# Who splits the softmax weights into high and low parts: ScalarE, GpSimd and VectorE in a two-layer attention kernel

## The reference, cut to what matters

```python
x = x + conv_attention(group_norm(x))      # layer 0: 6 heads of 64, relative positions by row and column
t = tokens(x)
t = t + causal_attention(layer_norm(t))    # layer 1: 6 heads of 64
t = t + ffn(layer_norm(t))                 # 384 -> 1536 -> 384, exact gelu, weights are Kronecker products
# both attentions, per head:
#   w = softmax(q @ k.T * scale + bias_or_mask);  out = w @ v;  then one output projection
```

## Time and profile before

| | |
|---|---|
| median of 3 runs | 3036.42 us (3030.33 to 3038.16) |
| the profiled execution, its own time | 3037.59 us |
| its span, first to last instruction | 3035.9 us |
| mean granted TensorE clock | 0.957 of full speed |
| busy share: PE, PEld, DVE, ACT, POOL | 89%, 52%, 73%, 58%, 59% |
| length of one image in the steady state | about 372 us |

### The profile page before, as it was taken

One profiled execution on the slowest core, in us unless ns is written; L12 is line 12 of the kernel. 1 busy time (PEld: TensorE's weight loads), 2 busy tenths in 40 slices (PEclk: granted clock), 3 DMA queues, 4 the chain that ended last, 5 costly groups with the idle time before them and its releaser, 6 DMA issues.

```text
span 3035.9 us, 68416 instructions
## 1 busy us (share of the span) xinstructions
PE 2700.3 (89%) x29020; PEld 1576.3 (52%) x29020; DVE 2223.7 (73%) x3769; ACT 1767.0 (58%) x2091; POOL 1781.9 (59%) x1181
## 2 busy tenths in 40 slices
PE   5899888999889988899989999899988999889995
PEld 3455544556446563465635655355553655535562
DVE  6786868767777777867777687686876868767684
ACT  5565645646556566564565655656555565555563
POOL 5374764737547375583756746466464665647464
PEclk8999999999999999999999999899999999999998
DMA  3000001000100001000010000100001000010000
GB/s 118 22 2 1 2 22 43 2 1 2 43 22 2 1 2 43 22 2 1 2 43 22 2 1 2 54 11 2 1 2 63 2 2 1 2 43 2 2 2 22
DMA packets 32751, 48.11 MB, mean 16 GB/s; under 512 B 5152, under 2 KB 32032, under 8 KB 32448
## 3 DMA queue, kind: packets, MB, share of 16 engines
q1 hardware_dynamic: 30944, 43.13, 4.3%
q10 hardware_dynamic: 1504, 0.61, 0.1%
HBM read 30.95 MB, written 12.58 MB: 14 GB/s over the span
## 4 chain that ended last, share of the span: by engine, by line
PE 42%; DVE 21%; POOL 16%; issue 13%; ACT 7%; DMA 0%; POOLq 0%; DVEq 0%; SPq 0%; ACTq 0%
PE ps L547 10%; POOL pl L995 8%; PE ps L881 6%; POOL ph L1038 5%; DVE mxp L951 5%; PE ps L671 4%; PE ps L842 4%; PE ps L851 4%; PE ps L806 4%; DVE pl L995 3%; ACT qa L655 2%; DVE stats L1115 2%; PE ps L844 2%; DVE x L1111 2%; PE ps L1090 2%
## 5 line engine op out<-in xcount | busy, mean ns | idle before, releaser
L995 POOL TENSOR_TENSOR pl<-p,ph 128x1024 f16<-128x1024 f32 x336 | 822.7, 2448 | 406.0 <-ACT ph L928 381.6
L951 DVE TENSOR_REDUCE mxp<-ps 128x1 f32<-128x512 f32 (+2 forms) x1344 | 777.4, 626 | 180.0 <-PE ps L806 172.2
L926 ACT ACTIVATE p<-ps 128x1024 f32<-128x1024 f32 (+1 forms) x672 | 644.1, 960 | 450.4 <-PE ps L851 444.1
L881 PEld LDWEIGHTS ps<-v,ph 128*128 128x128 f16 x9600 | 517.7, 98 | 133.0 <-issue 42.6
L995 DVE TENSOR_TENSOR pl<-p,ph 128x1024 f16<-128x1024 f32 (+1 forms) x336 | 426.5, 1269 | 214.4 <-POOL ph L1038 209.2
L881 PE MATMUL ps<-v,ph 128*128 128x65 f16 (+1 forms) x9600 | 541.9, 195 | 22.7 <-DVE pl L995 14.9
L881 PE MATMUL ps<-v,pl 128*128 128x65 f16 x4800 | 519.3, 194 | 0.0
L881 PEld LDWEIGHTS ps<-v,pl 128*128 128x128 f16 x4800 | 452.8, 100 | 0.0
L851 PE MATMUL ps<-qc,kc 65*128 65x512 f16 (+3 forms) x1344 | 388.5, 371 | 0.0
L686 POOL TENSOR_TENSOR v<-o,v 128x384 f16<-128x384 f32 x128 | 113.2, 889 | 444.6 <-ACT o L682 444.6
L928 ACT ACTIVATE ph<-p 128x1024 f16<-128x1024 f32 x336 | 355.2, 1057 | 10.7
(11 more groups left out here) (189 smaller groups left out, 5244.7 us busy)
## 6 DMA issues: line engine op xcount, KB each, us to landing
xin<-in_x SPq DMA_DIRECT2D x8, 1536.0 KB, 7.0
x<-in_x SPq DMA_DIRECT2D x8, 1536.0 KB, 8.0
out<-x SPq DMA_DIRECT2D x16, 768.0 KB, 3.6
qc<-rowt SPq DMA_DIRECT2D x96, 2.0 KB
o<-in_L_conv_qkv_w SPq DMA_DIRECT2D x2, 576.0 KB, 10.3
p<-in_L_conv_qkv_w SPq DMA_DIRECT2D x1, 576.0 KB, 11.4
x<-in_L_attn_Wq SPq DMA_DIRECT2D x1, 576.0 KB, 12.1
x<-in_L_attn_Wk SPq DMA_DIRECT2D x1, 576.0 KB, 13.0
```

The source lines that it names most:

```text
L881: mm = nc.tensor.matmul(m.ps[:, 6 + half % 2, c0:c0 + w], e, v, start=(first and n == 0), stop=(g in self.last_of_half and n == len(work) ...
L926: nc.scalar.activation(m.p32[:, i % RING, :, 0:w], m.ps[:, 2 * (i % 2):2 * (i % 2) + 2, 0:w], ACT.Exp, scale=SCALE).then_inc(s["exp"], 1)
L951: nc.vector.reduce_max(m.mxp[:, h % 2, kh, qt:qt + 1], m.ps[:, bank, 0:w], AX.X).then_inc(s["free"], 1)
L995: engine.tensor_tensor(m.pl[:, i % RING, :, 0:w], m.p32[:, i % RING, :, 0:w], m.ph[:, i % RING, :, 0:w], ALU.subtract).then_inc(sem, 1)
```

## The change

ScalarE makes the high part of every group. GpSimd makes the low part of all of an even group and of the first key tile of an odd group. VectorE makes the low part of the second key tile of an odd group. The semaphores `hi_act` and `hi_pool` become one, `hi`; readers of an odd group's low part wait for `pl_pool` and for `pl_dve`.

```diff
     def wait_hi(self, eng, i):
-        name = "hi_act" if self.even(i) else "hi_pool"
-        eng.wait_ge(self.s[name], self.s.at(name, i // 2 + 1))
+        eng.wait_ge(self.s["hi"], self.s.at("hi", i + 1))
     def wait_lo(self, eng, i):
-        name = "pl_pool" if self.even(i) else "pl_dve"
-        eng.wait_ge(self.s[name], self.s.at(name, i // 2 + 1))
+        eng.wait_ge(self.s["pl_pool"], self.s.at("pl_pool", i + 1))
+        if not self.even(i):
+            eng.wait_ge(self.s["pl_dve"], self.s.at("pl_dve", i // 2 + 1))
...
-    def high_part(self, eng, i, copy, sem):
+    def high_part(self, act, i):
...
-        copy(m.ph[:, i % RING, :, 0:w], m.p32[:, i % RING, :, 0:w]).then_inc(sem, 1)
+        self.nc.scalar.activation(m.ph[:, i % RING, :, 0:w], m.p32[:, i % RING, :, 0:w], ACT.Copy).then_inc(self.s["hi"], 1)
...
-            if self.even(i):
-                self.high_part(act, i, lambda out, in_: nc.scalar.activation(out, in_, ACT.Copy), s["hi_act"])
+            self.high_part(act, i)
...
-    def low_part(self, eng, engine, i, sem):
+    def low_part(self, eng, engine, i, sem, part):
...
-        engine.tensor_tensor(m.pl[:, i % RING, :, 0:w], m.p32[:, i % RING, :, 0:w], m.ph[:, i % RING, :, 0:w], ALU.subtract).then_inc(sem, 1)
+        engine.tensor_tensor(m.pl[:, i % RING, part, 0:w], m.p32[:, i % RING, part, 0:w], m.ph[:, i % RING, part, 0:w], ALU.subtract).then_inc(sem, 1)
...
-                self.low_part(dve, self.nc.vector, i - 1, self.s["pl_dve"])
+                self.low_part(dve, self.nc.vector, i - 1, self.s["pl_dve"], 1)
...
-            if self.even(i):
-                self.low_part(pool, nc.gpsimd, i, self.s["pl_pool"])
-            else:
-
-                self.high_part(pool, i, lambda out, in_: nc.gpsimd.tensor_scalar(out, in_, 1.0, 0.0, ALU.mult, ALU.add), self.s["hi_pool"])
+            self.low_part(pool, nc.gpsimd, i, self.s["pl_pool"], slice(0, 2) if self.even(i) else 0)
```

More of the change, by code:

```diff
@@ L693 @@
 class Attention:
-    COUNTS = (dict(scores=48, exp=48, hi_act=24, hi_pool=24, pl_dve=24, pl_pool=24, pv=48, use=116, free=116, combined=6, nm=6, row=96, recip=12,
+    COUNTS = (dict(scores=48, exp=48, hi=48, pl_dve=24, pl_pool=48, pv=48, use=116, free=116, combined=6, nm=6, row=96, recip=12,
                    out=12, ot_hi=6),
-              dict(scores=36, exp=36, hi_act=18, hi_pool=18, pl_dve=18, pl_pool=18, pv=36, use=84, free=84, combined=6, nm=6, row=96, recip=12,
+              dict(scores=36, exp=36, hi=36, pl_dve=18, pl_pool=36, pv=36, use=84, free=84, combined=6, nm=6, row=96, recip=12,
                    out=12, ot_hi=6))
@@ L905, in tensor @@
         self.use(pe, self.tail[1])
-    def high_part(self, eng, i, copy, sem):
+    def high_part(self, act, i):
         m, w = self.m, self.cols(i)
-        eng.wait_ge(self.s["exp"], self.s.at("exp", i + 1))
+        act.wait_ge(self.s["exp"], self.s.at("exp", i + 1))
         if i >= RING:
-            eng.wait_ge(self.s["pv"], self.s.at("pv", i - RING + 1))
-        copy(m.ph[:, i % RING, :, 0:w], m.p32[:, i % RING, :, 0:w]).then_inc(sem, 1)
+            act.wait_ge(self.s["pv"], self.s.at("pv", i - RING + 1))
+        self.nc.scalar.activation(m.ph[:, i % RING, :, 0:w], m.p32[:, i % RING, :, 0:w], ACT.Copy).then_inc(self.s["hi"], 1)
     def ot_high(self, act, u):
```

## The result

The changed kernel takes 2981.11 us (median of six runs; one of the six, at 3863.61 us, was disturbed), and the kernel before, run beside it, 3033.05 us. The ratio is 0.984, with a 95% interval of 0.982 to 0.986. That is 51.9 us less, where I forecast 27.5. The span of the profiled execution fell by 57.5 us, from 3035.9 to 2978.4, and the mean granted clock rose from 0.957 to 0.968.

What follows compares the result with a forecast made beforehand. TensorE was taken as the bound, losing 126 us waiting for VectorE, itself held up by GpSimd. Terms of -3.3 us in seven images and -4.4 in the last gave -27.5 from 3037.6, 3010.1, as median 3009; range 2978 to 3048.

Steps and rivals of the forecast that it cites:

- steps 13 and 21: Layer 0, each with a row behind an odd low part: VectorE's shorter low part saves 2 x 0.54, -1.1 us.
- step 3: Layer 0, TensorE waiting on VectorE: half of the odd low part leaves VectorE, saving 0.54 us.
- steps 5 and 6: Layer 0: line 988 no longer waits behind GpSimd's high part before step 5's row, 1.0 us; clock 1.7 more as bound.
- the units: Layer 0: the copy of line 405 starts 0.37 us later behind the high part, six times an image, +2.2 us.
- steps 27 to 36: Layer 0's normalisation: ScalarE becomes the bound at 5.55 us a pair, 28.35 us against 27.36, +1.0 us.
- step 37: Layer 0, step 37 to 38: the row is done in time, 6.25 us becomes 4.18, -2.1 us.
- steps 38 to 46: Layer 0's last head: exponential and high part on ScalarE take 2.03 us, TensorE's own pace, so priced at nothing.
- layer 1, first two heads (steps 0 to 11): The low part no longer waits for a high part from an occupied GpSimd: -2.0 us, bounds 0 and -3.
- layer 1, last heads: ScalarE's added high parts cost time, half of 1.9 us of waiting for VectorE's low part goes: +0.2 us.
- rival (b): Row stalls vanish: half of TensorE's 126 us of waits for VectorE and the slow clock stretch go; 2983 us, chance 0.17.
- rival (c): VectorE and GpSimd start an odd group's halves together, VectorE is held 1.06 us; slower, 3046, at worst 3083; chance 0.18.
- (d): GpSimd's even low part still holds the row; gains fail, ScalarE's costs come: 3047 us, or 3039; chance 0.20.

Runs made afterwards that it cites:

- unit_first: The changed kernel, with ScalarE's copy of a unit moved ahead of the odd group's high part: 2943.32 us, 0.971 of the kernel before; run again, 2939.70 us.
- group5: The kernel before, with only the high part of group 5 in layer 0 moved from GpSimd to ScalarE: 3020.74 us, 0.996 of before.
- layer1_only: The kernel before, with the whole change made in layer 1 alone: 3013.83 us, 0.994 of before.
- hi_only: The changed kernel, with odd low parts whole on VectorE as before; ScalarE still makes all high parts: 3011.92 us, 0.993 of the kernel before.
- pool_all: The changed kernel, with all low parts on GpSimd and none on VectorE: 3004.13 us, 0.992 of the kernel before.
- norm_pool: unit_first, with layer 0's high parts of groups 27, 29, 31, 33, 35 on GpSimd and their low parts whole on VectorE: 2988.38 us, 0.987 of before.

## Why the prediction was right, and where it was wrong

The direction was right, the size was not: 52 us less against 27.5, and 2981 us against 3009. That 2981 is just inside the range (2978 to 3048) is luck, as two errors of opposite sign met. One step failed in kind: steps 13 and 21, -1.1 in the sum, measured +3.2. Without this loss (unit_first) the time is 2943, far under the range. The other terms came out 8 us an image better than the sum had them, mostly because it left the slow stretches behind steps 5 and 37 out of the sum (2.6 us), took layer 1's gain too low (1.9), had the stages between the attentions at nothing (1.5) and charged steps 27 to 36 for what they didn't cost (1.0). Term by term, in us of a steady image:

| term of the sum | forecast | measured |
|---|---|---|
| step 3 | -0.54 | -0.53 |
| steps 5 and 6 | -1.0 | -2.7 |
| steps 13 and 21 | -1.1 | +3.2 |
| the units | +2.2 | +1.7 |
| steps 27 to 36 | +1.0 | 0.0 |
| step 37 | -2.1 | -2.55 |
| steps 38 to 46 | 0 | -1.1 |
| layer 1, first two heads (steps 0 to 11) | -2.0 | -3.3 |
| layer 1, steps 12 to 26 | 0 | -0.6 |
| layer 1, last heads | +0.2 | +0.2 |
| the stages between the attentions | 0 | -1.5 |

**Step 5, and its clock.** The cause was right: group5 moves that one high part and gets step 5 at 4.48 us and step 6 at 2.47. Mis-sized was the rest of the term: I named the slow stretch of the earlier trace rows as a bound, 1.7 us, and left it out of the sum. It came: 1.0 and 1.7 are the 2.7 measured. The timeline and the window after the change:

```profile
856.06 2.13 POOL L994 TENSOR_TENSOR pl<-p,ph 128x1024 f16<-128x1024 f32 x1 [1.36 <-ACT ph L912]
...
856.61 1.60 DVE L985 TENSOR_TENSOR mxp<-mxp 128x8 f32<-128x8 f32 x1
858.24 0.17 DVE L987 TENSOR_SCALAR nm<-mxp 128x8 f16<-128x8 f32 x1
...
859.06 0.22 PE L811 MATMUL ps<-ident,nm 128*8 128x128 f16 x1 [1.30 <-DVE mxp L950]
...
853.00:863.00 10.00, 8.70 (x103) 5.07 (x102) 7.72 (x13) 6.35 (x7) 5.06 (x5) 1.00 0.01 2
```

VectorE's combination still waits behind GpSimd's even low part (1.60 us), as rival (b)'s counter-argument had it, but the scaling no longer waits (0.17). TensorE stands 1.30 us instead of 1.87, and the granted clock over the 10 us is 1.00, so all of it at 2.4 GHz, instead of 0.83. Step 6 falls from 3.64 us to 2.47 by this. The same holds of step 38 (2.86 to 2.00), behind the stop of step 37, which I hadn't priced at all; there the granted clock had also been 0.83 over 10 us before the change. That a shorter stop keeps the clock up is read from these places. The length of one stop doesn't settle it, as step 21 shows.

**Steps 13 and 21.** This step of the prediction failed. I subtracted 0.54 us twice and wrote against rival (c) that the maxima ahead of the low part in VectorE's queue let GpSimd's half get well ahead. GpSimd's half was not the danger, but its next even low part, 2.14 us. Before, VectorE had started ahead of it by 0.28 us, and my own term for the units, 0.37 us later, was larger than this lead. I had priced that shift for TensorE's maxima alone and not carried it on to VectorE's low part.

The hold costs 1.4 us in step 13 (3.84 to 5.23 in six images) and 1.4 in step 21 (3.95 to 5.34). In four images step 21 took a further 1.4 to 1.7 us at the lower clock: of the windows below, the third image's and the fourth's, the first is at 0.83 and the second at 1.00, though TensorE had stopped for 1.97 us in both. That was one of my signs of being wrong, a new stop with a low clock behind it. In the third image step 13 fell instead, from 7.47 us. unit_first gives all of this back.

```profile
903.00:913.00 10.00, 8.03 (x79) 4.59 (x77) 6.91 (x11) 5.16 (x7) 3.29 (x2) 0.83 0.01 3
1267.70:1277.70 10.00, 8.03 (x103) 5.21 (x102) 8.56 (x13) 6.57 (x8) 3.29 (x2) 1.00 0.01 2
```

So rival (c) is real at two steps an image, by another partner than the one it named, and it is nowhere near deciding the sign.
The Trainium skill, page "SBUF — State Buffer", section "Who interferes with whom", says that the order of issue decides who is blocked. By that rule the trace agrees: VectorE 0.07 us behind took 2.62 us, and 0.06 us ahead took 0.69.

**The units.** The copy came 0.36 us later (0.37 forecast). Five of the six even steps behind it took 0.34 us more; step 14 has nothing waiting and took the same (2.54, 2.55).

**Steps 27 to 37.** ScalarE did become the bound; its timeline in steps 33 to 35, and the window over steps 33 to 36, after the change:

```profile
946.24 0.80 ACT L460 ACTIVATE lT<-xin,small 128x512 f32<-128x512 f32 x1
947.07 0.63 ACT L466 ACTIVATE xin<-lT 128x512 f16<-128x512 f32 x1
947.60 1.01 ACT L926 ACTIVATE p<-ps 128x1024 f32<-128x1024 f32 x1
948.64 1.06 ACT L912 ACTIVATE ph<-p 128x1024 f16<-128x1024 f32 x1
949.60 1.00 ACT L926 ACTIVATE p<-ps 128x1024 f32<-128x1024 f32 x1
...
944.00:954.00 10.00, 10.00 (x137) 6.42 (x135) 7.82 (x14) 9.82 (x12) 9.69 (x7) 1.00 0.01 2
```

The mechanism was right, the term too large. Neighbouring instructions of ScalarE can overlap in the records: the exponential at 949.60 starts 0.10 us before the high part ahead of it ends, so a high part adds less than its 1.06 us. From one exponential to the next it is 2.00 us, and an odd step takes 3.37 us where I had added a full 1.06 to 2.46 and got 3.52. A pair is 5.37 us where I had 5.55, and the ten steps take 27.34 us (27.37 before). Steps 37 and 38 gained as TensorE had the row ready in time; the row of step 37 waits for nothing after the change. Steps 39 to 46 go at ScalarE's pace of 2.00 instead of 2.03.

**Layer 1.** Both the low part that came late and its wait were right, but I read one instance and took its 1.95 us, where the first two heads held more such steps: they fell from 24.03 to 20.67 us. This is above my upper bound of 3. layer1_only shows that this gain stands by itself, and hi_only (20.62 us for these steps) that it comes from the high part and not from the split. VectorE's low part waited 209 us for GpSimd's high part before, over the whole span, and now waits 183 us for ScalarE's, so the waits of VectorE in total don't show this gain; the steps do.

**The stages between** gave 0.3 to 1.1 us an image that I had at nothing. No experiment takes them apart. In layer1_only the part from layer 0 to layer 1 is absent, so it hangs on layer 0's half of the change; more isn't shown.

**The rivals.** The time fell on rival (b)'s 2983, and partly for its reason: the four waits of the earlier trace rows for VectorE's maxima, scaling and low part, 126 us, are down to 73, and the clock held at step 5. But the row stalls of steps 13 and 21 got longer and were not gone; with unit_first, where they take 3.7 us each, the time is 2943, and the waits before the row are 36.7 us, under the 40 that I had forecast. Rivals (c) and (d) as told did not come.

## What to carry to other kernels

When work moves between engines, follow the shift on through each queue behind it: here a copy of 0.6 us that came 0.36 us late cost 38 to 48 us of 3000 (5.8 us an image, 4.1 of it since VectorE then lost a race to GpSimd at two places). The rows of the kernel before held the warning: a lead of 0.28 us, and one image in which it was lost. Steps should be read over all images, not in one. Where two engines hold each other up, look up in the trace which starts first and by how much, and order the late engine's producers so that the one on the critical path wins (putting that one copy first was worth nearly as much as the whole change). Beside a partner that worked without a gap, even an instruction of eight elements was late by 7.5 us (pool_all).

## What the runs showed of the hardware

- The start that decides is close: VectorE 0.06 us ahead of GpSimd took 0.69 us for its 512-wide low part, and 0.07 us behind 2.62 us. In the kernel before, 0.28 us ahead it took 1.22 us for the 1024-wide one, and 0.08 us behind 3.14.
- An instruction of VectorE can be held by more than one of GpSimd. With GpSimd busy without a gap, eight elements took 7.66 us, from inside the first pair of low parts to the end of the second (pool_all).
- The scaling of eight float32 to float16, with one SBUF input, was held as well: 2.06 us in norm_pool beside a GpSimd low part of 2.14, and 2061 ns at most in the kernel before.
- A stop of TensorE of 1.30 us left the granted clock at 1.00 over 10 us; after one of 1.87 us it was 0.83. Its length alone doesn't decide: the stop of step 21, 1.97 us in each of seven images, came with a stretch at the lower clock in four of them and with none in three.
